# Order of the two score units in each pair on TensorE: transposed unit first, straight unit second

## The reference

```python
x = x + 0.5 * ffn(layernorm(x), w1, b1, w2, b2)      # weights made ternary, gelu, 256 -> 1024 -> 256
x = x + attention(layernorm(x), Wq, Wk, Wv, Wo)      # 16 heads of 16, rotary positions, causal softmax
x = x + 0.5 * ffn(layernorm(x), w1, b1, w2, b2)
# in attention, per batch element and head:
scores = q @ k.T / 4; scores = where(causal, scores, -inf)
out = softmax(scores) @ v; return concat(out) @ Wo.T
```

## Time and profile before

| | |
|---|---|
| median of 3 runs | 605.15 us (605.0 to 605.78) |
| the profiled execution | 606.82 us, of which the span of instructions 605.1 us |
| granted clock of PE, mean | 0.993 of full speed |
| PE busy | 567.5 us (94%) |
| DVE busy | 458.6 us (76%) |
| ACT busy | 345.2 us (57%) |
| POOL busy | 229.8 us (38%) |

### The profile page before, as it was taken

One profiled execution on the slowest core, in us unless ns is written; L12 is line 12 of the kernel. 1 busy time (PEld: TensorE's weight loads), 2 busy tenths in 40 slices (PEclk: granted clock), 3 DMA queues, 4 the chain that ended last, 5 costly groups with the idle time before them and its releaser, 6 DMA issues.

```text
span 605.1 us, 17855 instructions
## 1 busy us (share of the span) xinstructions
PE 567.5 (94%) x6596; PEld 497.1 (82%) x6596; DVE 458.6 (76%) x928; ACT 345.2 (57%) x610; POOL 229.8 (38%) x446
## 2 busy tenths in 40 slices
PE   1899999999689999999999999999878999999997
PEld 1789999999668888888888888888665788899996
DVE  5977777778687988879878798877572777777764
ACT  1765455556236666866667666576556655554542
POOL 6373333333646353542545435434131033333310
PEclk9999999999889999999999999999999999999999
DMA  6630000000867666655575555766500011111111
GB/s 204 213 111 6 0 0 0 0 0 4 242 181 207 184 188 187 166 149 174 165 200 166 149 165 159 206 165 168 153 2 3 1 36 35 35 35 35 35 35 36
DMA packets 71142, 63.45 MB, mean 105 GB/s; under 512 B 4130, under 2 KB 64322, under 8 KB 71106
## 3 DMA queue, kind: packets, MB, share of 16 engines
q1 hardware_dynamic: 69922, 62.81, 35.9%
q10 hardware_dynamic: 1184, 0.14, 0.2%
HBM read 33.03 MB, written 29.36 MB: 103 GB/s over the span
## 4 chain that ended last, share of the span: by engine, by line
PE 82%; DVE 9%; DMA 3%; ACT 2%; POOL 2%; issue 1%; SPq 1%; DVEq 0%; POOLq 0%
PE bank L173 18%; PE bank L534 17%; PE bank L1062 13%; PE bank L670 7%; PE bank L1057 6%; PE bank L1118 5%; PE bank L1193 4%; PE bank L1158 3%; PE bank L156 2%; PE bank L1121 2%; PE bank L1131 2%; DVE mx L860 2%; DVE g_lo L257 1%; DMA w1f<-w1t 1%; PE bank L1181 1%
## 5 line engine op out<-in xcount | busy, mean ns | idle before, releaser
L860 DVE TENSOR_REDUCE mx<-bank 128x2 f32<-128x512 f32 (+1 forms) x192 | 118.4, 681 | 32.8 <-PE bank L1062 32.7
L534 PE MATMUL bank<-w2q,g_hi 128*128 128x256 f32 x512 | 124.4, 284 | 1.8 <-DVE g_lo L257 1.5
L240 ACT ACTIVATE g<-bank,b1c 128x512 f32<-128x512 f32 x128 | 88.1, 691 | 64.7 <-PE bank L173 61.5
L534 PE MATMUL bank<-w2q,g_lo 128*128 128x256 f32 x512 | 122.5, 280 | 0.0
L982 ACT ACTIVATE probs<-bank 128x512 f32<-128x512 f32 x192 | 111.1, 597 | 11.7 <-PE bank L1062 4.1
L534 PEld LDWEIGHTS bank<-w2q,g_hi 128*128 128x128 f32 x512 | 96.4, 188 | 3.6 <-DVE w2q L372 1.3
L534 PEld LDWEIGHTS bank<-w2q,g_lo 128*128 128x128 f32 x512 | 96.4, 188 | 0.6
L312 POOL TENSOR_TENSOR res<-res,b2h 128x1024 f32 (+1 forms) x16 | 38.4, 2400 | 133.2 <-DVE xn L147 128.6
L257 DVE TENSOR_TENSOR g_lo<-g,g_hi 128x512 fp32r<-128x512 f32 x128 | 82.6, 686 | 3.1
L173 PE MATMUL bank<-xt_hi,w1q 128*128 128x512 f32 x240 | 76.9, 402 | 2.0 <-DVE xt_lo L167 2.0
L173 PE MATMUL bank<-xt_lo,w1q 128*128 128x512 f32 x240 | 76.1, 398 | 0.0
(11 more groups left out here) (129 smaller groups left out, 1172.6 us busy)
## 6 DMA issues: line engine op xcount, KB each, us to landing
qk_slots<-parts SPq DMA_DIRECT2D x32, 384.0 KB, 3.7
q<-qk_slots SPq DMA_DIRECT2D x32, 384.0 KB, 4.0
k<-qk_slots SPq DMA_DIRECT2D x32, 384.0 KB, 4.8
qk_slots<-parts SPq DMA_DIRECT2D x32, 256.0 KB, 3.4
res<-x SPq DMA_DIRECT2D x8, 512.0 KB, 3.6
qk_slots<-parts SPq DMA_DIRECT2D x32, 128.0 KB, 3.2
out<-res SPq DMA_DIRECT2D x8, 512.0 KB, 2.9
w1f<-w1t SPq DMA_DIRECT2D x2, 512.0 KB, 6.4
```

Source lines behind the costliest of these rows:

```text
L240: nc.scalar.activation(g[:, f, :], of[:], ACT.Gelu, bias=b1c[:, f:f + 1]).then_inc(g_ready, 1)
L534: last = nc.tensor.matmul(to[:, 0:D], part[:, f, t * P:(t + 1) * P], w2q[:, f, :], start=f == 0 and part is g_hi, stop=f == FC - 1 and par ...
L860: nc.vector.tensor_reduce(o, i, AX.X, ALU.max).then_inc(s_done, 1)
```

## The change

In `step` of PE's attention stream, the two calls in the loop over units change places. Nothing is added or removed.

```diff
@@ -1198,10 +1198,10 @@
                 closing = p.known and p.p == BATCH - 1
                 last = p.known and p.p == BATCH
                 for n in range(6 * h, 6 * h + 6):
+                    if p.has(0):
+                        T(p, n)
                     if p.has(1):
                         S(p, n)
-                    if p.has(0):
-                        T(p, n)
                     if closing and n == 1:
                         hidden_ahead(pe, 0)
                     if closing and n == 7:
```

## The result

The changed kernel is slower by a third of a percent: 608.03 us median (606.55 to 609.21, 15 runs) against 605.47 us for the kernel before in the same comparison (604.97 to 607.99, 15 runs). The ratio is 1.0033, 95% interval [1.0024, 1.0043], so +2.0 us with an interval of 1.5 to 2.6 (the two medians lie 2.6 us apart). The forecast was +2.3 and 607.4.

What follows compares the result with a forecast made beforehand. PE was taken to set the pace, busy 240.29 of 245 us in steady attention. Terms 0.3 - 0.2 + 1.65 + 0.6 + 0.25 - 0.3 = +2.3 us on the 605.15 median gave 607.4, range 605.3 to 608.8.

Steps and rivals of the forecast that it cites:

- looped pairs, 15 halves: The six pairs in looped halves whose length counts: H + 3.80 against 3.78, 15 x 0.02 = +0.3 us.
- unrolled pairs: The six pairs in six unrolled halves, period 0 half 1 included: 3.80 against 3.84, 6 x -0.04 = -0.2 us.
- XT of the five odd halves: Half 1 of odd looped periods: later maxima delay statistics, low_att and XT by 0.33, 5 x 0.33 = +1.65 us.
- MT of periods 13 and 14: Half 0 of both periods: MT waits for POOL, fed by the last maximum; whole delay paid, 2 x 0.29 = +0.6 us.
- period 0, half 0: T starts where it did, S stands behind it; one S unit of 0.28 no longer done ahead: +0.25 us.
- period 14, half 1: T unit now fills 0.28 of the fourth S unit's 0.67 wait for DVE; the output projection comes earlier: -0.3 us.
- rival D: First exponential waits for the whole copy and the sequencer adds 0.1; every half 0.15 longer, +3.2 us, 610.6; chance 0.07.
- A: The main forecast, XT pays: 607.4 us, with bounds from 606.2 to 608.8; chance 0.70.
- the last S unit offers 4.07: DVE's last maximum: last S unit starts about 3.47, plus 0.45 matmuls and 0.15 to DVE's start; tail 0.33 later.
- rival C: ACT's ring holds PE; ACT's work behind the exponentials comes 0.2 earlier in 14 halves 1, -2.8 us, time 603.5; chance 0.06.
- B: The swap evens out: pairs run at 3.70 without any wait, -2.0 against +2.2 us, time 605.3; chance 0.15.
- E: PE reorders units within its 64-deep window, so program order means nothing and time stays 605.15 us; chance 0.02.

Runs made afterwards that it cites:

- e5: All pairs but the first of each half swapped (S0 T0 T1 S1 T2 S2 ...), against the kernel before: 614.74 us, ratio 1.0145.
- e2: T unit first everywhere but in half 1 of the odd looped periods, against the kernel before: ratio 1.0010.
- e8: Kernel before with DVE's statistics behind low_xt, T first only in period 0 half 1, periods 11 and 12, half 1 of 13 and 14: ratio 0.9980.
- e1: T unit first only in half 1 of the odd looped periods, against the kernel before: ratio 1.0028.
- e7: T unit first everywhere and DVE's statistics moved behind low_xt, against the kernel before: ratio 0.9980.
- e6: Old unit order, DVE's four statistics of odd periods moved from ahead of low_att to behind low_xt, against the kernel before: ratio 0.9980.
- e3: Only the first pair of each half swapped (T0 S0 S1 T1 S2 T2 ...), against the kernel before: ratio 1.0008.
- e9: Kernel before with statistics behind low_xt, only first pair swapped in most halves, all pairs in two, none in two: 603.18 us against 605.65, ratio 0.9954.

## Why the prediction was right

The place, the chain and the direction were those that the prediction named; the size was too high, by 0.9 us against the traces. Its terms, beside what the two traces show over periods 0 to 14:

| term | forecast | measured |
|---|---|---|
| looped pairs, 15 halves | +0.3 | +0.16 |
| unrolled pairs | -0.2 | -0.26, and -0.32 in period 0 half 1 |
| XT of the five odd halves | +1.65 | +1.36 |
| MT of periods 13 and 14 | +0.6 | +0.55 |
| period 0, half 0 | +0.25 | +0.25 |
| period 14, half 1 | -0.3 | -0.32 |
| sum | +2.3 | +1.42 |

*The pairs.* H + 3.80 was forecast and is what both kinds of halves have; the third T unit was put at H + 1.27 and starts at 1.28. The way there was in part luck. Before the change this unit started 0.30 behind the unit ahead of it, against 0.28 for a unit without a wait, so its wait was 0.02 and not 0.05; after it the step is 0.35, a wait of 0.07. The two errors cancel. The bound by which the first exponential waits for the whole copy did not come true: it starts 0.48 behind the copy's start, as in the earlier trace rows. That bound was also put too low: a start 0.11 later would have made a half 0.02 + 0.11 = 0.13 longer, the figure used in rival D, and not 0.08. Summed as they stand, the bounds of A end at 608.7, not 608.8.

*XT.* The tail of the maxima was taken as 0.33 later and is 0.28 later. The step that was off is "the last S unit offers 4.07": it ends at H + 3.87 (282.69 in the trace) and the last maximum starts 0.09 behind it, at 3.96, which is also start plus five paces. The 0.15 between an S unit's end and the maximum was read from the first maximum of a half, and holds there alone: it is 0.15 again in the changed kernel, but in e5 the third maximum of the half starts 0.04 behind the end of its S unit, though DVE had idled for 0.25:

```profile
283.36 0.39 PE L1062 MATMUL bank<-k,q 99*64 99x256 bf16 x4
```

(the last of these matmuls ends at 283.74, the maximum starts at 283.78). What makes the first one later is not known. With start plus pace alone the term is 5 x 0.29 = 1.45. That is also the sum that the prediction drew from the Trainium skill ("VectorE: DVE Perf Modes", section "The DRAIN you can't avoid"), and it comes nearer than 1.65, yet not for its reason: the six maxima do not follow at their full length of 0.68. They still take 3.68 us, one every 0.60, and each starts before the one ahead has ended.

*Period 0, half 1* was counted among the pairs at -0.04 and gave -0.32. It is the mechanism of rival C in the one half where it applies. The attention output of an earlier period does not exist yet, so ACT goes from the exponentials straight to the copies of the rotated projections, DVE's work behind them waits for ACT, and PV waits for DVE. The row of PV in that half before:

```profile
194.81 0.64 PE L1118 MATMUL bank<-probs,v_pad 128*32 128x256 f32 x8 [0.68 <-DVE att L900]
```

With ACT done 0.32 earlier (exponentials end at H + 4.23 in place of 4.55), the half is 0.32 shorter. The rival was judged by the steady half only. e2 and e8 show the 8.30 us again.

*The other rivals.* B is wrong: the pairs are 3.80 and not 3.70, the third T unit still waits for ACT. C's time was added up wrongly, though nothing hangs on it: B's 605.3 less 2.8 is 602.5, not 603.5. D is wrong: neither the copy nor the sequencer adds 0.1. E is wrong: if T and S units could pass each other, e5 would have cost nothing; the four orders give pairs of 3.74, 3.78, 3.80 and 4.02 us.

*The timed runs against the traces.* The timed ratio says +2.0 us (1.5 to 2.6), the traces +1.42, just below that interval. The granted clock on record for each run helps here. The profile of the changed kernel, with one stretch of 3.4 us, has a mean clock of 0.996, that of the kernel before, with 6.8 us, 0.993. Runs with like clocks compare as follows (for the kernel before, the runs of the later comparisons):

| mean granted clock | changed, mean us (runs) | before, mean us (runs) | difference |
|---|---|---|---|
| 0.996, 0.997 | 606.82 (4) | 605.31 (30) | +1.5 |
| 0.992 to 0.994 | 608.19 (3) | 606.02 (34) | +2.2 |
| 0.991 or less | 608.15 (8) | 607.63 (11) | +0.5 |

Weighted by the changed kernel's runs that is +1.1, with few runs behind it, but no more than the traces say. What stands out is the share of runs with the lowest clocks: eight of 15 against 11 of 75. So the traces' 1.4 us is the better figure for the order, and the rest of the 2.0 seems to go with time at the lower clock, of which the forecast said nothing. That the forecast of 2.3 lies so near the timed 2.0 is in part luck: terms that were 0.9 too high, and 0.6 that was not thought of.

*What stays open.* Whether the change itself makes the lower-clock stretches more frequent was not tested. The kernels ran in different comparisons, and the counts are small: e1, which has most of the price, has no run of twelve at 0.991 or less, and e7, with T first everywhere, has five.

## What to carry to other kernels

When two engines are fed by one in turns, the order decides whose chain starts late, and what it costs is read at the place where that chain is next waited for, not in the loop itself: here the loop was 0.02 us longer, and a wait that begins 2.3 us behind it, in five halves of thirty, made the price. If the delayed engine has work between its chain and the awaited result that nobody needs soon, move that work first (e6, e7); then the order is free, and a single swapped pair can be better than all or none (e3, e9). In a ring of two buffers, count the units that stand between an entry and its reuse: here four of them gave no wait, three one of 0.02 to 0.07 us, and two one of 0.30 us on PE (0.40 on its weight load).

## What the runs showed of the hardware

Kernels that are the same up to that place have a stretch at 1.2 GHz at the opening of the attention that is 3.4 us long in five traces and 6.8 in six, and three traces have one more of 3.4 us near 442 or 452 us. The longer stretch at the opening cost about 1.2 us more than the shorter; the extra one cost 0.9 us in e7 (19.51 us for period 14 against 18.61 in the changed kernel). PE had idled for the load of k before the first, 2.8 to 3.7 us, and the length of that wait does not tell which stretch follows (2.80 us in e6 with the short one, 2.82 in e7 with the long one). It had idled 1.4 us for POOL and 0.5 us for DVE just before or at the start of the later one; the changed kernel has the same two waits there and its clock stays at the full level. A single profile of each kernel can so hide a change of 1.4 us; the looped halves, away from these stretches, repeat to 0.02 us between the two traces of the kernel before.
